# A routing product on GpSimd in place of VectorE, and a GpSimd normalisation that adds a negated mean

## What is computed

```python
x = x + 0.5 * ffn(layernorm(x))     # phase 0
x = x + retention(layernorm(x))
x = x + 0.5 * ffn(layernorm(x))     # phase 1

def ffn(src):
    attn = softmax_attention(src, 16 heads of 8) @ Wo + bo
    x = layer_norm(src + attn, ln1_g, ln1_b)
    keys = (x @ router_w + router_b)[..., 0]
    expert_idx = remainder(floor(keys), 4)
    ff_out = the one expert of expert_idx: relu(x @ W1[e] + b1[e]) @ W2[e] + b2[e]
    return layer_norm(x + ff_out, ln2_g, ln2_b)
```

## Time and profile before

| | us |
|---|---|
| median of 3 runs | 948.08 |
| lowest, highest | 946.7, 950.37 |
| the profiled execution's own time | 951.38 |
| its span (first to last instruction) | 949.3 |

### The profile page before, as it was taken

One profiled execution on the slowest core, in us unless ns is written; L12 is line 12 of the kernel. 1 busy time (PEld: TensorE's weight loads), 2 busy tenths in 40 slices (PEclk: granted clock), 3 DMA queues, 4 the chain that ended last, 5 costly groups with the idle time before them and its releaser, 6 DMA issues.

```text
span 949.3 us, 26557 instructions
## 1 busy us (share of the span) xinstructions
PE 828.5 (87%) x8607; PEld 625.8 (66%) x8607; DVE 762.0 (80%) x1935; ACT 665.3 (70%) x1370; POOL 568.6 (60%) x801
## 2 busy tenths in 40 slices
PE   4899899999999688479999979999999999996883
PEld 3566666666666688457877856666666666666883
DVE  5688788888897877669898864888888888978775
ACT  2588788888887477435454554988888888874774
POOL 5135667576665667627777682265765757565666
PEclk9999999999999999889999995999999999998998
DMA  9995698000004667230000000000000000046671
GB/s 288 380 417 82 164 412 362 12 11 22 11 23 134 187 197 236 76 87 2 0 0 0 1 1 2 2 13 12 11 22 11 22 11 11 24 143 201 193 240 48
DMA packets 41812, 96.64 MB, mean 102 GB/s; under 512 B 5224, under 2 KB 25470, under 8 KB 37260
## 3 DMA queue, kind: packets, MB, share of 16 engines
q1 hardware_dynamic: 36236, 83.11, 27.1%
q0 software_dynamic: 5504, 12.63, 3.8%
HBM read 43.64 MB, written 53.13 MB: 102 GB/s over the span
## 4 chain that ended last, share of the span: by engine, by line
PE 45%; DVE 20%; issue 18%; POOL 13%; DVEq 1%; ACT 1%; DMA 1%; POOLq 0%; ACTq 0%
DVE mx L1357 9%; PE duo L576 8%; PE duo L632 7%; PE duo L569 3%; POOL out L1930 3%; DVE qk_lo L1346 2%; PE duo L882 2%; POOL x_mid L1930 2%; PE duo L641 2%; PE duo L861 2%; POOL xs L1922 2%; PE duo L570 2%; PE duo L870 2%; PE duo L723 2%; PE duo L840 2%
## 5 line engine op out<-in xcount | busy, mean ns | idle before, releaser
L1357 DVE TENSOR_REDUCE mx<-duo 128x4 fp32r<-128x1024 f32 x256 | 312.2, 1220 | 73.5 <-PE duo L576 68.4
L1047 ACT ACTIVATE probs<-duo 128x1024 f32<-128x1024 f32 x256 | 263.3, 1029 | 58.3 <-PE duo L582 53.7
L576 PE MATMUL duo<-stacks 32*128 32x256 f32 x1024 | 133.6, 338 | 36.3 <-DVE mx L1357 27.3
L632 PE MATMUL duo<-probs,v_st 128*32 128x256 f32 x2048 | 140.3, 392 | 0.3
L582 PE MATMUL duo<-q_st,stacks 32*128 32x256 f32 x1024 | 131.5, 335 | 0.1
L576 PEld LDWEIGHTS duo<-stacks 32*128 32x128 f32 x1024 | 80.7, 191 | 72.6 <-issue 32.7
L1826 POOL TENSOR_TENSOR a_ln<-mv_ln,eps_ln 128x2 f32<-128x2 f32 x32 | 6.3, 197 | 145.3 <-DVE mv_ln L1322 145.1
L569 PE MATMUL duo<-qk_hi,sel_r 128*128 128x256 f32 x256 | 83.0, 345 | 7.6 <-DVE qk_lo L1346 7.6
L632 PEld LDWEIGHTS duo<-probs,v_st 128*32 128x32 f32 x2048 | 54.1, 110 | 41.5 <-issue 3.4
L723 PE MATMUL duo<-w,xs 128*128 x608 | 77.0, 281 | 4.3 <-DVE hidden L1524 1.8
L582 PEld LDWEIGHTS duo<-q_st,stacks 32*128 32x128 f32 x1024 | 77.9, 188 | 1.4 <-ACT probs L1047 0.5
(11 more groups left out here) (219 smaller groups left out, 2178.8 us busy)
## 6 DMA issues: line engine op xcount, KB each, us to landing
x_sorted<-ret SPq DMA_DIRECT2D x2, 17476.0 KB, 49.0
wbuf<-w_pack SPq DMA_DIRECT2D x38, 512.0 KB
ret<-x_sorted SPq DMA_DIRECT2D x22, 257.0 KB
stacks<-x_sorted SPq DMA_DIRECT2D x12, 257.0 KB
wside<-w_pack SPq DMA_DIRECT2D x38, 66.0 KB
w_pack<-wbuf SPq DMA_DIRECT2D x2, 1024.0 KB, 8.4
decay_rows<-prow SPq DMA_DIRECT2D x1, 1536.0 KB
xs<-x_sorted SPq DMA_DIRECT2D x4, 257.0 KB
```

The source lines that it names most:

```text
L576: return pe.matmul(score_bank[h % 2][:, t * SEQ:(t + 1) * SEQ], q_st[r:r + 32, g, t * P:(t + 1) * P], k_st[r:r + 32, g, :], start=True, st ...
L632: last = pe.matmul(pv_bank[32 * j:32 * j + 32, cols], v_st[:, t, h, :], probs[:, h % RING, t, :], start=(t == 0), stop=(t == TT - 1))
L1047: act.activation(probs[:, h % RING:h % RING + 2, :, :], duo_now[:].rearrange("p (n t q) -> p n t q", n=2, t=TT), ACT.Exp, scale=SCALE).the ...
L1357: dve.tensor_reduce(rows, score_duo[:].rearrange("p (n t k) -> p n t k", n=2, t=TT), AX.X, ALU.max, negate=True).then_inc(max_done, 1)
```

## The change

The router's product of every batch except the last of a phase moves from VectorE's `route` step 0 to GpSimd, as `route_product`, between `make_x1` and `own_row`; it waits for `x1` and for the preceding batch's reduction, and it counts on the same semaphore. GpSimd's `normalise` no longer subtracts the mean and multiplies, but adds the negated mean (computed by one more small multiply in `rstd`, into the scratch tile `c`) and multiplies; a new semaphore `neg_mean` orders the two. A constant tile of -1 is set at the start. Line numbers in the text are those of the kernel before.

```diff
--- before.py
+++ after.py
@@ -192,6 +192,7 @@
         eps_col = sb("eps_col", [P, 1])
         half_root = sb("half_root", [P, 16])
         eps_ln = sb("eps_ln", [P, TT])
+        minus_one = sb("minus_one", [P, TT])
         eps_gn = sb("eps_gn", [P, 16])
 
         s_nat = sb("s_nat", [P, TT, DM])
@@ -312,6 +313,7 @@
 
         prep_ln, ln1, ln2 = sem("prep_ln"), sem("ln1"), sem("ln2")
         seed = {"ln2": sem("seed_ln2")}
+        neg_mean = {"prep": sem("neg_mean_prep"), "ln1": sem("neg_mean_ln1")}
         ln_sem = {"prep": prep_ln, "ln1": ln1, "ln2": ln2}
 
         sT_ps, sT_ready = sem("sT_ps"), sem("sT_ready")
@@ -1596,7 +1598,7 @@
                             maximum(i, 2 * p)
                         if p == 0:
                             if live(i - 3, base):
-                                for n in range(3):
+                                for n in range(0 if is_last(i - 3, base) else 1, 3):
                                     route(i - 3, base, n)
                         elif p == 1:
                             if live(i - 3, base):
@@ -1790,6 +1792,7 @@
         def _(pool):
             pool.memset(half_root[:], -0.5)
             pool.memset(eps_ln[:], LN_EPS)
+            pool.memset(minus_one[:], -1.0)
             pool.memset(eps_gn[:], GN_EPS * RV)
             pool.memset(ones_wide[:], 1.0).then_inc(set_pool, 1)
             pool.wait_ge(set_pool, 1)
@@ -1821,18 +1824,22 @@
 
             def rstd(b, which, steps=1):
 
+
                 s, done = ln_scratch[which], ln_sem[which]
                 pool.wait_ge(done, b * 8 + 4)
                 pool.tensor_tensor(s["a"][:], s["mv"][:, :, 1], eps_ln[:], ALU.add).then_inc(done, 1)
+                if steps == 1:
+                    pool.tensor_tensor(s["c"][:], s["mv"][:, :, 0], minus_one[:], ALU.mult).then_inc(neg_mean[which], 1)
                 pool.wait_ge(done, b * 8 + 5)
                 pool.tensor_tensor(s["rstd"][:], s["a"][:], half_root[:, 0:TT], ALU.pow).then_inc(done, steps)
 
-            def normalise(b, which, src, dst):
+            def normalise(b, which, src, dst, nth):
 
                 s, done = ln_scratch[which], ln_sem[which]
                 pool.wait_ge(done, b * 8 + 6)
+                pool.wait_ge(neg_mean[which], nth)
                 for t in range(TT):
-                    pool.tensor_scalar(dst(t), src(t), s["mv"][:, t, 0:1], s["rstd"][:, t:t + 1], ALU.subtract, ALU.mult).then_inc(done, 1)
+                    pool.tensor_scalar(dst(t), src(t), s["c"][:, t:t + 1], s["rstd"][:, t:t + 1], ALU.add, ALU.mult).then_inc(done, 1)
 
             def add_bo(b, base):
 
@@ -1854,6 +1861,13 @@
                 pool.tensor_tensor(xt1[:], n1[:], wide(g1_b), ALU.mult).then_inc(x1_ready, 1)
                 pool.wait_ge(x1_ready, b * 2 + 1)
                 pool.tensor_tensor(x1_all[:, b - base, :, :], xt1[:], wide(b1_b), ALU.add).then_inc(x1_ready, 1)
+
+            def route_product(b, base):
+
+                pool.wait_ge(x1_ready, b * 2 + 2)
+                wait(pool, router, (b - 1) * 8 + 2)
+                pool.tensor_tensor(rprod[:].unsqueeze(1), x1_all[:, at(b, base), :, :],
+                                   rw_b.unsqueeze(1).unsqueeze(1).to_broadcast([P, 1, TT, P]), ALU.mult).then_inc(router, 1)
 
             beats = [0]
 
@@ -1889,8 +1903,9 @@
                     elif live(i - 2, base):
                         rstd(i - 2, "ln1")
                         wait(pool, x1_ready, (i - 2) * 2)
-                        normalise(i - 2, "ln1", lambda t: y1[:, t, :], lambda t: n1[:, t, :])
+                        normalise(i - 2, "ln1", lambda t: y1[:, t, :], lambda t: n1[:, t, :], i - 1 - base // BATCH)
                         make_x1(i - 2, base)
+                        route_product(i - 2, base)
                         own_row(i - 2, base)
                     if live(i, base):
                         place_v(i, 1)
@@ -1904,7 +1919,7 @@
                         rstd(i + 2, "prep")
                         wait(pool, sT_ps, i + 2)
                         wait(pool, resid_ready, i + 2)
-                        normalise(i + 2, "prep", lambda t: xs[:, i + 2 - base, t, :], lambda t: s_nat[:, t, :])
+                        normalise(i + 2, "prep", lambda t: xs[:, i + 2 - base, t, :], lambda t: s_nat[:, t, :], i + 3)
                         if i == -2:
                             fills()
                         add_bo(i + 2, base)
```

## The result

The changed kernel takes 935.28 us (median of 4 runs, 933.7 to 946.9) against 948.95 us of the kernel before beside it (4 runs, 946.7 to 950.37). The ratio is 0.9884 with a 95% interval of 0.9836 to 0.9932; it is taken over all the runs and is not the quotient of the two medians (0.9856). Run again later, in rounds beside the kernel before, the changed kernel took 934.98 against 951.09 us, 0.9848 (0.9797 to 0.99). It is faster by 1.2 to 1.5%; the forecast was 0.8%. Medians here are of all runs; ratios, and times put at an equal clock, leave out the runs over 1.5% above the fastest of their kernel.

What follows compares the result with a forecast made beforehand. It took VectorE, 0.29 us late for p1's maximum, as the steady limit, with ScalarE and GpSimd close behind. Steady turns 3.6, four places 1.5 and starts 2.6 gave 7.7 us: median 940.4 from 948.08; own range 937 to 944, whole 936 to 964.

Steps and rivals of the forecast that it cites:

- VectorE's slot: Steady turns, around p0: without the product VectorE starts the maximum of p1 earlier; 0.15 us per turn, 3.6 us, bounds 0 and 7.0.
- the burst of p2 next meets the exponential: TensorE's burst of p2 can start only 0.12 us after ScalarE's exponential of p1, which limits the gain to 0.17 us.
- rival C: Burst of p2: neither limit binds, so the full 0.29 us per turn is gained, 11.1 us in all, 937.0; chance 0.07.
- Behind p2, nothing gives it back: Later slots of the turn: the maxima of p3 and p4 start right behind VectorE's own work, so they move with p2.
- Four places where the product stood on the chain: Last full turn and drain of both phases: the product is on the chain; about 0.38 us each, 1.5 us, bounds 0.5 and 1.8.
- GpSimd's sum: GpSimd per turn: 1.13 us added, 1.78 us saved by the new normalisation at 350 ns, 0.65 us shorter in net.
- Rival A: GpSimd's normalisation: the new form is not faster, the transposes slip, 18.5 us slower, 966.6 (962 to 971); chance 0.20.
- The new wait: VectorE's reduction now waits for GpSimd's product, which would be done with over 2 us to spare.
- Starts: First batch, cleared-rows wait and second phase's start: normalisation on the chain, 0.74 us gained per pair; 2.6 us, bounds 1.5 and 3.8.

Runs made afterwards that it cites:

- act_more: The changed kernel with one more small activation on ScalarE between the exponentials of p0 and p1; 935.85 us (one run).
- before_again: The kernel before, unchanged, run once more for its slots; 952.91 us (one run).
- product_alone: The kernel before with only the routing product moved to GpSimd, the old normalisation kept; 961.59 us beside 950.64, ratio 1.0117.
- form_alone: The changed kernel with the routing product back on VectorE, the new normalisation kept; 949.8 us beside 950.64, too scattered for an interval.
- form_again: form_alone repeated on another chip: the changed kernel with the routing product back on VectorE; 952.55 us beside 952.81, ratio 1.0015.
- step5_again: Repeat of the changed kernel with the routing step that makes the masks moved from slot p2-p3 to the one before; 939.21 us, ratio 0.9872.

## Why the prediction came out as it did

The direction, the mechanism and its place were right; the time is 5 us below the forecast, 0.7 us outside the range's lower end by the median (by the ratio 0.9884 of 948.08, which is 937.1, inside it). By its own steps:

- *VectorE's slot, 0.15 us per turn, 3.6 us.* The mechanism holds: p1 became bound by its scores, 0.54 us behind the burst. The size was wrong. The step "the burst of p2 next meets the exponential", with its lag of 0.12, failed: p0-p1 gained 0.28, the full limit of VectorE, and p1-p2 gave nothing back. That is rival C, to which I gave 0.07. act_more shows why: a lag seen once is no minimum. In the earlier trace rows the burst followed a late exponential by chance, and in before_again it did not: there the exponential of p0 ends 0.39 us ahead of the burst of p1. The first trace of before shows it too: over its turns i = 4 to 13 that distance is 0.10 to 0.14 us in eight and 0.36 and 0.39 in two, and the burst of p1 starts 1.35 to 1.36 us behind the start of p0's maximum in all ten. From i = 5 to 14 nine turns took 152.05 us before and 149.84 after, 0.24 each, so 24 are 5.8 us.
- *p5 to p7.* "Behind p2, nothing gives it back" missed 0.04 us: the counts (L1433) now take 0.33 us instead of 0.15, since they meet GpSimd's two-input multiplication L1861 (202.47 to 203.20) where they met the old normalisation before. p5-p6 grows by 0.19, and p6-p7 returns 0.15 of it. In the one turn in which the counts took 0.62 us (236.17 to 236.80, with L1861 up to 236.78) p5-p6 is 2.70.
- *Four places where the product stood on the chain, 1.5 us.* The last turn (i = 14 to 15) fell from 17.48 to 16.96 in the first phase, 0.52, against 0.25 of a steady one; the drain behind it (to the last maximum) by 0.25. Beyond the steady gain that is about 0.5 per phase, 1.1 in all: less than forecast, within its bounds. The drain's part goes with the product (13.68 us in product_alone, 13.94 in form_alone, 13.95 before, though once 15.39 in before_again). In the last turn p0-p1 saves 0.36 and p2-p3 saves 0.26, and the second of these is the form's: form_alone has it with the product on VectorE, and comes to 17.02 for that turn.
- *GpSimd's sum, -0.65 us per turn.* From the row addition's statistics to the end of the normalisation GpSimd took 11.03 us before (from 189.47 to 200.50) and 10.41 after: -0.62. Two terms were off and met: the form takes 449 ns and not 350, four times 0.1 us less gain; but the negated mean adds next to nothing, 0.02 us from L1830 to the power's start (0.30 after, 0.28 before), where 0.15 each was forecast. The product costs 0.82 spacing, as forecast.
- *Rival A* fell by the form's duration. Its mechanism was right: at the old 795 ns the transposes do slip. product_alone adds only the product, 0.83, and with the slack of 0.25 that I read, the turn should have grown by 0.58; it grew by 0.48 (the mean of i = 5 to 13 went from 16.89 to 17.37), so the slack was 0.35, and the kernel lost 11 us. GpSimd's chain to the transposes is started by VectorE in the preceding turn (L1322), so the 0.28 that p0-p1 saves on the way does not bring it forward: it is waited away again in p2-p3, which grows by that much more than the turn.
- *The new wait* costs nothing, with over 3 us to spare, as forecast.
- *Starts, 2.6 us.* Measured: the second phase's first maximum came 0.65 us sooner behind retention (9.17 to 8.52), where 1.48 was forecast for the pair (the distance is from the start of the last retention output, L1669, to the first maximum; product_alone has 9.15 and form_alone 8.51, so it is the form's), and the first batch about 0.5, with as much scatter between executions. The term is 1.2 us, under half the forecast of 2.6.
- *What no term had: the stall.* I read the normalisation at 96.23 as work behind a wait for the cleared rows. The row before it shows 3.40 us of idle time in front of the scatter, with no releaser. It went away with the positions in GpSimd's stream, 4.5 us. No term of a forecast made from the kernel's work alone could have held it.

Together: 5.8 + 1.1 + 1.2 = 8.1 us, where 7.7 were forecast, and 4.5 us of the stall: 12.6, against 11 to 12 at equal clock. That 8.1 comes so near to 7.7 is in part luck: the steady turns gave 2.2 us more than forecast, the other two terms 1.8 less. That the two halves depend on each other was in the forecast only by way of rival A: neither half alone gains (1.0117; 1.0015), although both have the stall shortened too (0.97 and 0.19 us), and both together give 0.985 to 0.988. The product frees VectorE and needs the room in GpSimd's chain that only the form gives; the form alone moves GpSimd's work against VectorE's small operations.

What stays open: why the stall depends on the position (that it has to do with fetching the instructions is only argued, no row shows a fetch). Why form_again and step5_again have single slots of 2.3 to 2.7 us, one of 3.1, at unchanged work: in one such slot of form_again (i = 4, p7-p0) the burst starts at its usual distance of 1.48 us, and the maximum behind it 0.34 us late, with VectorE idle for 0.74 us. Of form_alone's lost time, 0.11 us per turn is seen in the bias addition; why it lost a further 0.1 to 0.3 in the repetition is not.

## What to carry to other kernels

Before work is moved to another engine, find its slack at each reader: here GpSimd had none towards the transposes, so the move cost 1.2% until another change shortened GpSimd's chain by more than the product lengthened it, and both together brought 1.2 to 1.5%. A lag between two engines, read at one place, is an upper bound of the least, not the least; look at the same slot over many turns, at several slots and, where possible, at two executions. Idle time with no releaser ("issue") in front of one instruction can come and go with any edit that shifts the stream; compare such rows before a gain is put down to the change.

## What the runs showed of the hardware

- On GpSimd a subtraction in a one-input instruction with two operations costs some 350 ns more per 128 columns than an addition (799 against 451 ns at 128 columns, 1225 against 557 at 256), as the first operation or the second; two pointers cost 150 ns more than two constants at 128 columns (451 against 299) and 113 at 256 (557 against 444).
- Small operations of VectorE are held up by some of GpSimd's. The counts, two inputs of 128x8, took 0.33 us (202.89 to 203.22) while GpSimd's L1861 ran to 203.20; alone they take 0.15. The Trainium skill (SBUF — State Buffer, section "SBUF: two separate sides") says that a port pair is shared by the two engines and is held for a whole instruction, also against a VectorE operation with two SBUF inputs when GpSimd's operation reads SBUF. These two ends, 0.02 us apart, agree, and so do those of all 24 counts that meet L1861 in the run, which take 0.23 to 0.62 us. The kernel before doesn't: there the counts took 0.15 us in the midst of the old normalisation (VectorE, then GpSimd), and so each time.

```profile
208.92 0.15 DVE L1431 TENSOR_TENSOR counts<-counts,masks 128x8 bf16<-128x8 bf16 x1
...
207.54 1.58 POOL L1835 TENSOR_SCALAR token_bufs<-token_bufs,mv_ln,rstd_ln 128x128 f32<-128x128 f32 x2 [0.18 <-POOL rstd_ln L1828]
```

  The mean of the counts is 292 ns after and 152 before. Why the old normalisation does not hold them up is not shown.
- A stall of 3.40 us in front of a scatter on GpSimd that 6 one-element instructions at the start of the stream take away (0.19 us).
- The same kernel's start of the second phase took 34.93 and 38.93 us in two executions. In the second the granted clock of TensorE was 0.50 to 0.56 (at or near the lower level) from 574 to 582, in the first it was back at 1.00 by 576.
